# Four transfers for X, base products in front of the router's logits, a residual as a matrix product

## The reference

```python
def _layernorm(x, axis=-1, eps=1e-05):
    m = jnp.mean(x, axis=axis, keepdims=True)
    v = jnp.var(x, axis=axis, keepdims=True)
    return (x - m) / jnp.sqrt(v + eps)
```

## Time and profile before

| | |
|---|---|
| runs (3) | 4417.88, 4421.68 (median), 4430.77 us |
| profiled execution | 4406.58 us, span 4404.8 us |
| PE busy | 3349.2 us (76%) |
| DVE busy | 2760.8 us (63%) |
| ACT busy | 2544.5 us (58%) |
| POOL busy | 1352.1 us (31%) |

### The profile page before, as it was taken

One profiled execution on the slowest core, in us unless ns is written; L12 is line 12 of the kernel. 1 busy time (PEld: TensorE's weight loads), 2 busy tenths in 40 slices (PEclk: granted clock), 3 DMA queues, 4 the chain that ended last, 5 costly groups with the idle time before them and its releaser, 6 DMA issues. The chain is left out here.

```text
span 4404.8 us, 53696 instructions
## 1 busy us (share of the span) xinstructions
PE 3349.2 (76%) x20182; PEld 1501.4 (34%) x20182; DVE 2760.8 (63%) x4514; ACT 2544.5 (58%) x4198; POOL 1352.1 (31%) x1221
## 2 busy tenths in 40 slices
PE   7597788989948988988887897899868696631126
PEld 4365122222211222222212565466544273211124
DVE  5123889989736665665565776477667132488886
ACT  2022377767858989989996776377533222312225
POOL 0401184010011010010001885388411403228880
PEclk9699799999979999999998999899989898775558
DMA  4101121110020010000000111011020021550000
GB/s 135 34 19 56 30 50 34 33 31 16 2 62 15 15 26 18 15 18 12 15 1 16 28 35 36 14 34 35 17 81 8 31 64 32 77 62 0 10 6 24
DMA packets 140026, 137.36 MB, mean 31 GB/s; under 512 B 42185, under 2 KB 104693, under 8 KB 139765
## 3 DMA queue, kind: packets, MB, share of 16 engines
q1 hardware_dynamic: 130612, 116.07, 12.0%
q0 software_dynamic: 8192, 16.79, 1.6%
q10 hardware_dynamic: 960, 1.05, 0.1%
HBM read 64.90 MB, written 33.82 MB: 22 GB/s over the span
## 5 line engine op out<-in xcount | busy, mean ns | idle before, releaser
L460 PE MATMUL PS<-t 50*128 50x512 bf16 (+2 forms) x3072 | 739.4, 398 | 187.6 <-ACT t L603 49.5
L722 DVE TENSOR_TENSOR t<-t 128x1536 f32<-128x1536 f32 (+1 forms) x384 | 586.3, 1596 | 129.7 <-ACT t L603 77.7
L585 ACT ACTIVATE t<-PS 128x512 f32<-128x512 f32 x1024 | 532.5, 602 | 230.9 <-PE PS L460 227.5
L640 DVE TENSOR_REDUCE t<-PS 128x1 f32<-128x1024 f32 x512 | 601.0, 1216 | 46.3 <-PE PS L452 42.3
L534 PE MATMUL PS<-t 128*9 128x512 f32 x4096 | 552.5, 612 | 12.6 <-DVE t L722 12.1
L605 ACT ACTIVATE t<-PS 128x1536 f32<-128x1536 f32 (+1 forms) x384 | 477.9, 1310 | 51.1 <-PE PS L460 35.9
L603 ACT ACTIVATE t<-PS 128x1536 f32<-128x1536 f32 (+1 forms) x384 | 476.9, 1310 | 37.4 <-PE PS L460 25.5
L460 PEld LDWEIGHTS PS<-t 50*128 50x128 bf16 (+2 forms) x3072 | 158.7, 94 | 970.8 <-ACT t L603 270.5
L452 PE MATMUL PS<-t 48*128 48x512 bf16 x1024 | 342.8, 406 | 47.2 <-DVE t L640 24.5
L1801 POOL TENSOR_TENSOR t<-t 128x512 f32<-128x512 f32 x128 | 159.7, 1269 | 576.6 <-ACT t L1666 576.1
L2617 PE MATMUL PS<-t 128*128 128x32 f32 x256 | 61.1, 403 | 344.6 <-ACT t L2663 280.9
(11 more groups left out here) (403 smaller groups left out, 6385.1 us busy)
## 6 DMA issues: line engine op xcount, KB each, us to landing
t<-scr SPq DMA_DIRECT2D x336, 64.0 KB
t<-t SPq DMA_DIRECT2D x128, 128.0 KB, 2.3
scr<-t SPq DMA_DIRECT2D x96, 128.0 KB
t<-t SPq DMA_DIRECT2D x16, 512.0 KB, 13.1
scr<-t SPq DMA_DIRECT2D x2, 2560.0 KB
t<-scr SPq DMA_DIRECT2D x16, 320.0 KB, 3.6
scr<-t SPq DMA_DIRECT2D x16, 320.0 KB, 2.7
t<-scr SPq DMA_DIRECT2D x48, 48.0 KB
```

What stands on the lines that cost most here:

```text
L460: return e.op.matmul(PS[:, bk, :], Kx[p // 4 % 2][lo:lo + rows, j, kb * 128:kb * 128 + 128], Qx[p // 4 % 2][lo:lo + rows, j, hf * 512:hf * ...
L585: e.op.activation(P[x % 4][:, 2 * hf + side, :], PS[:, bank((what, p, k, side, hf)), :], ACT.Exp, scale=S8).then_inc(*PW.up((p, k, side, hf)))
L640: e.op.tensor_reduce(MX[p % 2][:, side, qc:qc + 1], PS[:, 2 * side:2 * side + 2, :].rearrange("p a n -> p (a n)"), AX, ALU.max).then_inc(* ...
L722: e.op.tensor_tensor(o, o, SGM[(12 * p + 3 * blk + ti) % 3][:, 0:nu, :], ALU.mult).then_inc(*DG.up((p, blk, ti)))
```

## The change

First stage: `load_x` issues one DMA for each batch of 8 rows, each with its own counter (`ROWS`), and the identity alone raises `LD`, "x". DVE no longer waits for `LD`. It waits for a batch's counter, takes its 8 statistics, a drain, and its 8 aggregates, and goes to the next batch. `norm_stage` hands the counters through; its other caller gives none and keeps the old path.

Last but one layer: PE's logits become a step "logits" of `order()` behind "base". ACT's `route_act` moves from "turned" to the end of batch 0's "u". The search copies the weights W once into `WE` with the expert ahead of the row, in the place of `CN`, and compares and sums in that layout. The residual leaves POOL: `res` is multiplied by the identity once on DVE ("scales"), which makes a diagonal matrix, and each chunk of "out" has a third product, XT's chunk by that matrix. This is so in `unit([3])` too. `XR` is gone, and DVE's wait for POOL with it.

```diff
+        def norm_dve(e, src, dst, eps, tag, counted=False, pieces=None):
+            if pieces:
+                for b in range(NB):
+                    e.wait_ge(pieces[b], "rows")
+                    for c in range(8 * b, 8 * b + 8):
+                        e.op.bn_stats(stats[:, c, :], src[:, c, :]).then_inc(*DV.up())
+                    e.wait_ge(DV)
+                    for c in range(8 * b, 8 * b + 8):
+                        e.op.bn_aggr(mv[:, c, :], stats[:, c, :]).then_inc(*DV.up())
...
             def dve(e):
-                if load:
-                    e.wait_ge(LD, "x")
-                norm_dve(e, src, dst, eps, tag, counted)
+                norm_dve(e, src, dst, eps, tag, counted, pieces)
...
+                    WE = flat(CN).rearrange("p (e c) -> p e c", e=8)
+                    then().tensor_copy(WE, W[:].rearrange("p c e -> p e c")).then_inc(*DV.up())
...
                             e.op.tensor_tensor(
-                                GE[:, k, :, :], W[:],
-                                TC[:, k, :].bitcast(F32).unsqueeze(1).broadcast_to([128, NC, 8]), ALU.is_ge).then_inc(
+                                GE[:, k].rearrange("p c e -> p (c e)").rearrange("p (e c) -> p e c", e=8), WE,
+                                TC[:, k, :].bitcast(F32).unsqueeze(2).broadcast_to([128, 8, NC]), ALU.is_ge).then_inc(
                                 *DV.up())
-                        then().tensor_reduce(cnt[:], GE[:].rearrange("p k c e -> p k e c"), AX, ALU.add).then_inc(
-                            *DV.up(("count", bit)))
+                        then().tensor_reduce(
+                            cnt[:], GE[:].rearrange("p k c e -> p (k c e)").rearrange("p (k e c) -> p k e c", k=3, e=8),
+                            AX, ALU.add).then_inc(*DV.up(("count", bit)))
...
                             if route:
                                 yield "base", 0, 0
+                                yield "logits", 0, 0
                                 yield "turned", 0, 0
...
                                 mix.zero_pool(e)
-                                e.wait_ge(GC)
-                                for j in range(NC // 4):
-                                    e.wait_ge(PO)
-                                    e.op.tensor_tensor(XR[:], chunk4(XN, j), bc3(res[:], 4), ALU.mult).then_inc(
-                                        *PO.up())
-                                    e.wait_ge(PO)
-                                    e.op.tensor_tensor(chunk4(X, j), chunk4(X, j), XR[:], ALU.add).then_inc(
-                                        *PO.up(("res", j)))
                                 e.wait_ge(DV, "picks")
...
-                            if route:
-                                next(steps)
                             e.wait_ge(GC)
...
-                                if what == "count":
+                                if what == "count" or what == "logits":
                                     next(steps, None)
...
+                                        if route:
+                                            e.wait_ge(DV, "scales")
                                         for q in range(4):
                                             cs = slice((4 * j + q) * 128, (4 * j + q + 1) * 128)
                                             for x in range(2):
-                                                t = e.op.matmul(PS[:, bk, q * 128:(q + 1) * 128], OU[:, x, cs],
-                                                                ow[:, x, :], start=x == 0, stop=x == 1)
+                                                e.op.matmul(PS[:, bk, q * 128:(q + 1) * 128], OU[:, x, cs],
+                                                            ow[:, x, :], start=x == 0, stop=False)
+                                            xs = t0 + cs.start
+                                            t = e.op.matmul(PS[:, bk, q * 128:(q + 1) * 128], XT[:, xs:xs + 128],
+                                                            res[:], start=False, stop=True)
...
-                                elif what == "turned" and route and b == 0 and jb == 1:
-                                    mix.route_act(e)
+                                    if what == "u" and route and b == 0:
+                                        mix.route_act(e)
...
+                                e.op.tensor_tensor(res[:], res[:], ident[:], ALU.mult).then_inc(*DV.up("scales"))
...
                                 elif what == "out":
-                                    if route:
-                                        e.wait_ge(PO, ("res", 2 * b + 1))
...
+                ROWS = [sig(f"x_in{b}") for b in range(NB)]
+
                 def load_x(e):
-                    e.op.dma_start(X[:], a["L0_attn_x"].rearrange("b (c p) f -> p (b c) f", p=128)).then_inc(
-                        *LD.up("x", 16))
+                    for b in range(NB):
+                        e.op.dma_start(X[:, 8 * b:8 * b + 8, :],
+                                       a["L0_attn_x"][b].rearrange("(c p) f -> p c f", p=128)).then_inc(
+                            *ROWS[b].up("rows", 16))
                     e.op.dma_start(ident[:], a["ident"]).then_inc(*LD.up("x", 16))
```

More of the change, by code:

```diff
@@ L180, in chunk4 @@
             return t[:, 4 * j:4 * j + 4, :]
-        def norm_dve(e, src, dst, eps, tag, counted=False):
-            if not counted:
+        def norm_dve(e, src, dst, eps, tag, counted=False, pieces=None):
[7 more added lines that the diff above has]
+                        e.op.bn_aggr(mv[:, c, :], stats[:, c, :]).then_inc(*DV.up())
+            elif not counted:
                 for c in range(NC):
@@ L186, in norm_dve @@
                 e.wait_ge(DV)
-            for c in range(NC):
-                e.op.bn_aggr(mv[:, c, :], stats[:, c, :]).then_inc(*DV.up())
+            if not pieces:
+                for c in range(NC):
+                    e.op.bn_aggr(mv[:, c, :], stats[:, c, :]).then_inc(*DV.up())
             e.wait_ge(DV)
@@ L241, in norm_stage @@
         def norm_stage(src, dst, eps, tag, turned=None, load=None, scale=None, bias=None, counted=False,
-                       pool=None, also_sp=None):
+                       pool=None, also_sp=None, pieces=None):
             def sp(e):
@@ L2073, in unit @@
                             mix.route_tiles(c1)
-                            XR = sb([128, 4, 128], c=c1)
                         else:
@@ L3001, in load_x @@
                     mix.zeros(e)
-                norm_stage(X, XN, 1e-5, "n0", XT, load_x, pool=mix.zero_pool)
+                norm_stage(X, XN, 1e-5, "n0", XT, load_x, pool=mix.zero_pool, pieces=ROWS)
                 def load_first(e):
```

## The result

The changed kernel took 4404.26 us (median of 20 runs, 4394.71 to 4418.01) beside 4421.94 for the kernel before (20 runs): ratio 0.9961 (changed over before, as everywhere below), 95% interval 0.9952 to 0.997. Forecast were 4407.7 and a range of 4398 to 4421. The profiled execution of the changed kernel, 4416.62 us with a span of 4414.4, is not a typical one. The stages can.

What follows compares the result with a forecast made beforehand. Bounds: load then DVE in the first stage; logits, base, rotation, Exp, then mostly DVE's search rounds in routing, and the sends' halt. Terms 5.9 + 7.9 + 7.7 - 7.5 = 14.0 us gained gave 4407.7 us, range 4398 to 4421.

Steps and rivals of the forecast that it cites:

- First stage: X in four transfers: DVE starts at 5.25 and ends at 13.9 instead of 19.82, 5.9 us gained.
- the page's fixed cost paid in series: First stage: about 2 us fixed per DMA; three more in series would take 6 us and leave no gain.
- Exp: Last but one layer's routing: base before logits, Exp behind v and u; DVE goes on at 3260.1, 7.8 us gained.
- first count: Start of the search: 7.8 + 0.58 - 0.45 = 7.9 us earlier.
- the old rotation would do as well: Routing: even with its old rotation DVE would wait for the Exp from 3255.2, so 7.8 us come anyway.
- The bound of 11: Exp term's upper bound: v at 2.4 GHz and the logits a third quicker, 11 us gained.
- Counting: Search: reduction 0.95 us, 0.58 less a round; 5.7 from ten rounds plus 2.0 from the clock, 7.7 us gained.
- both slow legs: Search legs behind steps 1 and 2 lost 1.75 us each to the clock; both back 3.5, 2.0 taken.
- Residual as a product: 16 more PE passes in each of four "out", 1.87 us lost each, 7.5 in all.
- rival 3: Halt catches the second "out" unfinished, leaving 5.6 us after the sends instead of 1.87: 10.3 gained, 4411; chance 0.08.
- Rival 5: Last but one layer: halt comes at the first send, moving up to 31 us of products; 17 slower, 4439; chance 0.07.
- The sum: Whole kernel: 5.9 + 7.9 + 7.7 - 7.5 = 14.0 us gained, 4407.7 by the median.

Runs made afterwards that it cites:

- The three comparisons: The changed kernel against the kernel before, measured three times: ratios 0.9961, 0.9982 and 0.9955.
- the three other part runs: The kernel before with only the search's layout, only the new order, or only the residual's product: ratios 0.9967, 0.9996 and 1.0001.

## Why the forecast was right, and where it was not

*First stage, 5.9 forecast, 6.4 in the profile.* The mechanism was right, the size a little off: the first piece released DVE at 4.49, not 5.25. (By the prediction's own rates the first piece is through at 4.4 and not 4.5.) The four queued 512 KB pieces landed 2.1, 1.8 and 1.8 us apart, ahead of DVE, which takes 2.2 for a batch, and the last at 10.2, no later than X as a whole before (10.8). The Trainium skill has in "DMA: Bandwidth & Descriptors", section Bandwidth, the rule of at least 1 MiB for a transfer for three quarters of peak, from DMAs issued by GpSimd. With the page's fixed cost paid in series, as the prediction estimated, nothing would have been left. The trace does not bear that out for these transfers, queued by SP.

*Exp, 7.8 forecast, 7.98 measured; first count 7.9 and 8.14.* Each term held: base 3.67, v 5.55 for 5.4 (its window has a granted clock of 0.66), the Exp released behind u. One sentence was wrong: that the old rotation would do as well. It took the old rotation at its old length, though it would now run wholly beside POOL's products. With the order alone DVE went on 6.6 us earlier and 2.3 were left at the stage's end. In the changed kernel, without POOL's products, the slip did no harm. The bound of 11 for this term is a little low by its own parts, which give some 12; nothing was decided by it.

*Counting, 7.7 forecast.* The reduction took 953 ns (0.95 forecast). The legs gave 9.2: both slow legs came back, 3.5 and not the 2.0 taken. But 1.4 was lost behind count 15, at 1.2 GHz, where two rank products took 1.22 and 1.06 instead of 0.70 and 0.59, and the apply 4.14 instead of 3.60. The windows show it, of the changed kernel and of before (the column ahead of the DMA share is the clock):

```profile
3348.20:3356.90 8.70, 6.17 (x15) 3.49 (x14) 5.52 (x19) 0.00 (x0) 0.00 (x0) 0.80 0.00 0
```

```profile
3355.90:3363.20 7.30, 4.77 (x15) 2.58 (x14) 5.06 (x18) 0.00 (x0) 0.00 (x0) 1.00 0.00 0
```

Net 7.8, as forecast, but by two errors that cancel. The 1.4 is not the search's price. Timeline of the first rank product behind count 15: before, with the search alone, with the residual alone:

```profile
3358.82 0.70 PE L950 MATMUL PS<-t 128*128 128x256 f32 x2 [2.53 <-DVE t L1081]
```

```profile
3290.59 0.70 PE L950 MATMUL PS<-t 128*128 128x256 f32 x2 [2.52 <-DVE t L1084]
```

```profile
3300.34 1.22 PE L950 MATMUL PS<-t 128*128 128x256 f32 x2 [2.53 <-DVE t L1081]
```

With the search's layout alone nothing is lost there (19.39 us from count 15 to "above", 19.40 before), and it gains 9.9, 2 more than forecast. With the old search the slow stretch comes with the residual's product (22.60, of which 1.8 are the product) and with the new order (21.07). So the other parts bring it in; why they do stays open.

*Residual as a product, 7.5 lost by forecast.* **This term failed.** The first "out" cost its 1.8. The second and third were to cost 3.7 and cost 8.7, the last 1.87 and cost 2.3 to 3.7: 13 to 14 in all. Two causes. The halt caught the second "out" unfinished, which is rival 3, to which I had given 0.08: it said 5.6 for this "out", and the score that starts at 3505.62 stands 34.0 us behind the last send where it stood 28.9, so 5.1. The other 3.4 are the third "out": half of it ran at 1.2 GHz, and it took 7.3 us instead of 3.8. Timeline of its start, changed and before:

```profile
3527.11 0.71 PE L2195 MATMUL PS<-t 128*128 128x128 f32 x4 [2.45 <-DVE t L2283]
...
3530.24 1.06 PE L2195 MATMUL PS<-t 128*128 128x128 f32 x4
```

```profile
3526.50 3.84 PE L2192 MATMUL PS<-t 128*128 128x128 f32 x32 [2.45 <-DVE t L2276]
```

The kernels without the product end 6.8 (residual on POOL) and 7.3 us (on DVE) sooner behind the last send, so that much of the 8.7 is the product's; the rest is not assigned. By the pair with and without it the four "out" cost 11.5, by the table 13 to 14, and the sum had 7.5. The step that failed is to price the second and third "out" by their passes at 2.4 GHz. Rival 5 did not come: PE ran freely for over 30 us behind the first send.

*The sum.* The stages gave 8.1 instead of 14.0, near rival 3's 10.3. The three comparisons gave 17, 8 and 20 us, about 15. The stage of the first layer's routing (0.5 to 3.1 shorter) and the rest at the end (up to 4.7 shorter) may hold 4 more, and the experts take 1.3 back; some 4 us are not found. (In the run with the first stage alone that layer's routing was also 3 to 5 us shorter than in the three other part runs, 190.9 against 194.0 to 195.7; the reason is not shown.) A stretch that no one touched differs by 11 us between two executions of one kernel, so two or three profiles can't find them. So the forecast time was met in part by luck: the residual's loss was put 4 to 6 us too small, and some 7 us of gain came from outside the stages of the sum, 4 of them placed above without their reason.

## What to carry to other kernels

When a step is taken off an engine that is not the bound, look at what it slows beside it: POOL's products, off the path themselves, doubled DVE's rotation (20.1 us, not 10.9), and what their removal was worth depended on the order: DVE went on 3.7 us earlier with the old order and 1.4 with the new one. A cheap product on PE is priced by what runs at its place (here the halt and a stretch at 1.2 GHz), not by its passes alone. And put the small operation that everyone waits for (the Exp) at the first slot in which its input is there, even at the price of a second table load.

## What was not expected of the hardware

The halt during indirect DMAs was absent on one chip: there the kernel before took 4270 us, and 4413 to 4422 in the four comparisons elsewhere, with the same 79.8 us for the first layer's 64 sends. Where it is, it took 65 + 49 + 30 us in the three stages. What brings it on, and whether it stays with a chip, was not tried. Beside POOL's two-operand products DVE's 128x1024 product took 2.17 us instead of 1.23, and its scaling 1.64 instead of 0.81.
